# Second GINE layer held turned through two products, with a third product that brings its rows back without their mean

## Chip, cores and metric

The kernel runs on one core of a Trainium2 chip. The metric is the device time of one execution in microseconds (us), the median of several runs. Engines are called as the profile calls them: PE (TensorE, with PEld for its weight loads), DVE (VectorE), ACT (ScalarE), POOL (GpSimd) and SP (SyncE).

## What is computed

Four residual graph layers run over 100000 nodes of 96 channels with 50000 edges; each ends in a layer norm without gain or shift. The change touches the last layer, and of it the second convolution:

```python
def _layernorm(x, axis=-1, eps=1e-05):
    m = jnp.mean(x, axis=axis, keepdims=True)
    v = jnp.var(x, axis=axis, keepdims=True)
    return (x - m) / jnp.sqrt(v + eps)

def _gine_conv(x, src, dst, e, W1, b1, W2, b2):
    msg = jax.nn.relu(x[src] + e)
    agg = jax.ops.segment_sum(msg, dst, num_segments=x.shape[0])
    h = x + agg
    h = jax.nn.relu(h @ W1 + b1)
    h = jax.nn.relu(h @ W2 + b2)
    return h
...
h = _gine_conv(x, src, dst, e, W00, b00, W01, b01)
h = jax.nn.relu(h)
h = _gine_conv(h, src, dst, e, W10, b10, W11, b11)
h = jax.nn.relu(h)
...
x = _layernorm(x + h)      # this x is the output of the layer norm before
```

## The kernel before

Nodes without an incoming edge need no sums, so the dense rows of a layer ("base" rows) can be computed from the features alone. Rows of nodes with incoming edges ("slots", one for each edge, sorted by destination) are computed again with their sums and scattered over the dense ones. The last convolution runs in three stages.

- **First slots stage** (`slot_rows "gine1_slots"`): the slots of the first convolution, beside the lower half of the dense rows of the second. The change leaves it alone.
- **Gather stage** (`edge_pass "gine2"`, line 436): POOL issues 392 indirect DMAs (line 516), each of which fetches 128 rows of `conv`; seven make one of 56 batches, five batches are ahead, and eight buffers exist. DVE adds the edge features (`join`, line 534), ACT applies relu (line 633), DVE chains the rows into running sums in PSUM (line 582, eight instructions a batch), ACT copies the sums out (line 1887), SP stores them. When the last batch is chained, PE and ACT make one row of corrections (lines 602, 648, 651), which POOL adds by an indirect DMA (line 1944). Beside this each engine runs a share of a job: the upper half of the dense rows of the second convolution, class `GineRows`.
- **Last slots stage** (`slot_rows "gine2_slots"`): `GineRows` over 49 batches of 1024 slots, and POOL scatters each finished batch into the output with eight indirect DMAs (line 985).

`GineRows` (line 1159) works on half batches of 512 rows, step q on each engine in program order. PE transposes four tiles of 128 rows (line 1146, tile `turned`), ACT copies them to SBUF (line 1124), PE multiplies by the first weights with 512 columns (line 1242, `hidden`), ACT applies bias and relu (line 1227), and PE multiplies by the second weights so that the rows come back upright (line 1154, `product`, four matmuls of 96 columns; the bias rides on a row of ones). DVE takes relu and adds the skipped features (line 1208, `product` in PSUM, `skip` in SBUF). For each batch of two halves the norm follows: DVE sums the rows (line 1029) and subtracts the mean in one instruction on 768 elements whose two tensor inputs are both in SBUF (line 1031), ACT squares (line 1070), DVE sums the squares (line 1037), ACT takes the root (line 1076), DVE inverts it (line 1046), and the rows are scaled: with `scaled_by_act` by eight ACT instructions (line 1063), else by one DVE instruction with both inputs in SBUF (line 1050). In the slots DVE first adds the features to the sums, both in SBUF (line 1132), in odd steps:

```python
        if q % 2:
            self.add(ph, dve, (q + 3) // 2)
```

Before it writes a rows buffer again, DVE waits in `left` until the scatter of four batches ago has landed. The order of a stage is what the code issues: for every batch each engine runs its own work and then the job's steps that `share` gives to that batch (104 steps over 56 batches here).

## Time and profile before

| | us |
|---|---|
| median of 3 runs | 13920.73 (13897.24 to 13924.33) |
| profiled execution, its own time | 13921.51 |
| its span | 13919.8 |
| gather stage, first gather to last | 12807.52 to 13313.30 |
| last slots stage, first scatter to last | 13388.21 to 13916.7 |

The times of the timeline are counted from the start of the span. The gather stage and the last slots stage are the last 1112 us of the program.

### The profile page before, as it was taken

How to read it: one execution, taken by the hardware profiler on the slowest of the kernel's cores; microseconds unless marked ns; L12 is line 12 of the kernel's file. 1: busy time of each engine (PE TensorE's matmuls, PEld its weight loads, DVE VectorE, ACT ScalarE, POOL GpSimd, SP SyncE). 2: the span in 40 equal slices, each digit the busy share in tenths (PEclk: the TensorE clock that was granted, in tenths of full speed). 3: DMA queues.
4: the chain of work that ended last, by engine and by line, in shares of the span. 5: the costliest groups of instructions: out<-in, count | busy, mean ns of one | idle time of the engine just before them, and what ended most of it. 6: DMA issues, size and time to landing. Idle time of an engine off the chain costs nothing. (4 is left out here: it accounts for less than half of the span.)

```text
span 13919.8 us, 114314 instructions
## 1 busy us (share of the span) xinstructions
PE 5477.0 (39%) x29175; PEld 4357.4 (31%) x29175; DVE 7700.5 (55%) x13539; ACT 4324.3 (31%) x11110; POOL 8089.8 (58%) x8280
## 2 busy tenths in 40 slices
PE   0000002100000000210003877776778888988876
PEld 0000002000000000210002666654556887766544
DVE  8880245444444444542256255676755778567753
ACT  0000011100000000110046565466655246654654
POOL 0567777777777777777733773177765000721767
PEclk9965555555555555555556767987789988999555
DMA  7300124434334334431257544444467788876743
GB/s 227 117 4 3 36 78 137 123 113 119 113 113 119 113 113 119 127 107 53 55 187 239 167 142 132 148 141 126 138 212 244 233 288 316 269 252 227 227 165 111
DMA packets 955756, 2071.60 MB, mean 149 GB/s; under 512 B 318458, under 2 KB 323856, under 8 KB 938977
## 3 DMA queue, kind: packets, MB, share of 16 engines
q1 hardware_dynamic: 689376, 1702.87, 35.4%
q0 software_dynamic: 265728, 361.43, 11.6%
q8 instruction: 241, 3.95, 0.1%
q14 instruction: 411, 3.36, 0.1%
HBM read 1251.36 MB, written 822.13 MB: 149 GB/s over the span
## 5 line engine op out<-in xcount | busy, mean ns | idle before, releaser
L720 POOL DMA_INDIRECT hop_raw<-hop_table,i_hop x2352 | 2219.6, 944 | 734.5 <-issue 693.0
L814 PE MATMUL hop_rows<-hop_chain,src_carries 128*128 128x96 f32 x12 | 4.3, 450 | 3023.8 <-DVE hop_chain L790 3023.8
L744 DVE TENSOR_TENSOR hop_rows<-hop_raw,hop_factors 128x672 f32<-128x672 f32 x336 | 289.9, 863 | 1494.4 <-DMA hop_raw<-hop_table,i_hop 1494.4
L822 ACT ACTIVATE hop_keeps<-src_inner 128x672 f32<-128x672 f32 x336 | 255.4, 762 | 2665.2 <-DVE hop_chain L790 2613.1
L516 POOL DMA_INDIRECT gine_raw<-x,i_near x392 | 379.1, 967 | 1177.4 <-POOLq L89 1058.2
L516 POOL DMA_INDIRECT cheb_raw<-cheb_table,i_cheb x784 | 817.4, 1043 | 244.9 <-issue 235.9
L814 PEld LDWEIGHTS hop_rows<-hop_chain,src_carries 128*128 128x128 f32 x12 | 3.0, 312 | 3025.1 <-issue 3025.1
L516 POOL DMA_INDIRECT cheb_raw<-x,i_near x392 | 446.4, 1139 | 510.0 <-POOLq L89 390.8
L516 POOL DMA_INDIRECT gine_raw<-conv,i_near x392 | 387.6, 989 | 603.6 <-POOLq L89 484.5
L1784 POOL DMA_INDIRECT own_raw<-x,i_dst x392 | 370.1, 944 | 505.3 <-POOLq L89 386.2
L1621 PE MATMUL cheb_base_product<-folded,cheb_base_turned_rows 97*128 97x292 f32 x1568 | 561.9, 514 | 177.1 <-ACT cheb_base_mixed L1580 177.1
L790 DVE TENSOR_TENSOR_SCAN hop_chain<-hop_keeps,hop_rows 128x672 f32<-128x672 f32 x336 | 521.9, 1553 | 11.6
L985 POOL DMA_INDIRECT out_dram<-gine_slots_ends_rows,dst_end x392 | 410.3, 1047 | 154.5 <-issue 119.1
L299 POOL DMA_INDIRECT x_and_map<-sort_dst_entry,src_map_end x392 | 393.6, 1004 | 129.1 <-issue 128.2
L516 POOL DMA_INDIRECT gcn_raw<-x,dst_other x392 | 382.6, 976 | 131.0 <-issue 115.6
L299 POOL DMA_INDIRECT x_and_map<-fold_entry,dst_map_end x392 | 381.0, 972 | 127.8 <-issue 127.0
L2000 POOL DMA_INDIRECT hop_sums<-hop_last_sums,src_end x392 | 383.8, 979 | 119.4 <-issue 119.4
L1621 PEld LDWEIGHTS cheb_base_product<-folded,cheb_base_turned_rows 97*128 97x128 f32 x1568 | 354.0, 237 | 299.8 <-ACT cheb_base_mixed L1580 188.7
L720 POOL DMA_INDIRECT hop_first_raw<-x_and_map,src_other x392 | 369.9, 944 | 131.6 <-issue 119.2
L720 POOL DMA_INDIRECT hop_last_raw<-hop_table,i_hop x392 | 373.5, 953 | 122.5 <-issue 119.2
L720 POOL DMA_INDIRECT hop_second_raw<-hop_table,i_hop x392 | 369.9, 944 | 124.9 <-issue 113.4
L720 POOL DMA_INDIRECT hop_ninth_raw<-hop_table,i_hop x392 | 370.0, 944 | 122.4 <-issue 115.8
(560 smaller groups left out, 22128.9 us busy)
## 6 DMA issues: line engine op xcount, KB each, us to landing
hop_res<-hop_table SPq DMA_DIRECT2D x336, 336.0 KB
hop_table<-hop_sums SPq DMA_DIRECT2D x336, 336.0 KB, 2.3
part<-cheb_put_mixed SPq DMA_DIRECT2D x49, 1168.0 KB
cheb_slots_ends_part<-part SPq DMA_DIRECT2D x49, 1168.0 KB, 7.6
start_x_x<-x_and_map SPq DMA_DIRECT2D x98, 400.0 KB, 4.2
x<-start_x_rows SPq DMA_DIRECT2D x98, 400.0 KB, 4.0
cheb_base_term<-x SPq DMA_DIRECT2D x98, 400.0 KB, 3.7
mid<-cheb_base_rows SPq DMA_DIRECT2D x98, 400.0 KB
```

The source lines that it names most:

```text
L299: pool.indirect_dma_start(out=self.node_map, out_offset=bass.IndirectOffsetOnAxis(ap=side.map_end[:, t:t + 1], axis=0), in_=self.entry[:, ...
L516: pool.indirect_dma_start(out=raw_rows[:, b % RAW, g, :], out_offset=None, in_=table, in_offset=bass.IndirectOffsetOnAxis(ap=index[:, t:t ...
L720: pool.indirect_dma_start(out=raw_rows[:, b % RAW, g, :], out_offset=None, in_=table, in_offset=bass.IndirectOffsetOnAxis(ap=index[:, t:t ...
L744: nc.vector.tensor_tensor(by_channel(b).rearrange("p c t -> p t c"), raw[:, b % RAW, :, :], spread(weights[:, at], C), ALU.mult).then_inc( ...
L790: nc.vector.tensor_tensor_scan(line(chain), line(keeps), rows[b % LINES], 0.0, ALU.mult, ALU.add)\
L814: nc.tensor.matmul(carried, side.carries[:, :], chain[:, (batches - 1) % LINES, :, EDGE - 1], start=True, stop=True).then_inc(s["carried"], 1)
L822: nc.scalar.activation(keeps[:, b % LINES, :, :], side.inner[:, b * EDGE:(b + 1) * EDGE].unsqueeze(1).to_broadcast([P, C, EDGE]), ACT.Copy ...
L985: pool.indirect_dma_start(out=table, out_offset=bass.IndirectOffsetOnAxis(ap=side.end[:, t:t + 1], axis=0), in_=self.wide_rows[:, m, g, :] ...
L1621: ins = nc.tensor.matmul(into[:, start:], self.turned_rows[0:rows, q % 2, j, c, :], self.k.folded[0:rows, power, start:MIX], start=(j == 0 ...
L1784: pool.indirect_dma_start(out=raw[:, b % RAW, g, :], out_offset=None, in_=table, in_offset=bass.IndirectOffsetOnAxis(ap=index[:, t:t + 1], ...
L2000: pool.indirect_dma_start(out=self.out, out_offset=bass.IndirectOffsetOnAxis(ap=ph.edge["side"].end[:, t:t + 1], axis=0), in_=ph.edge["sum ...
```

## The change

Both later stages now use a new class, `CentredGineRows`; the dense rows of the lower half keep `GineRows`. After `hidden`, PE multiplies again with 512 columns, with the second weights as the stationary operand, so that the result stays turned (`second`, 96 x 512). ACT applies the second bias and relu (line 1323, `second_rows`). A third product (line 1154 again, four matmuls) brings the rows back upright, multiplied by `k.centring`, the identity less 1/96, which takes off each row's mean. The skipped features come out of a layer norm, so their mean is zero, and DVE adds them to the PSUM product with a plain add (line 1298). The row sum and the subtraction of the mean on DVE (lines 1029 and 1031) are gone. In the gather stage the scaling moves from eight ACT instructions to one DVE instruction (line 1050); in the slots ACT keeps it. Transposes run three steps ahead in place of two, loads three batches ahead in place of two, and in the gather stage `turned` and `hidden` have one PSUM bank each (`fronts=1`). In the slots the add of line 1132 moves to the start of the even step, ahead of the wait for the scatter.

```diff
+class CentredGineRows(GineRows):
+    signals = GineRows.signals + ("second", "bent")
+    LEAD = 3
...
+        self.steps = range(-3, 2 * self.count + self.tail)
...
+    def centre(self, ph, dve, i): pass
...
+    def vector(self, ph, dve, q):
+        i, m = q // 2, q // 2 % self.DEPTH
+        if q % 2 == 0:
+            self.add(ph, dve, q // 2 + 2)
+        if 0 <= q < 2 * self.count:
+            if q % 2 == 0 and i >= self.DEPTH:
+                self.left(ph, dve, i - self.DEPTH)
+            g0 = q % 2 * 4
+            self.landed(ph, dve, i)
+            dve.wait_ge(self.sem(ph, "product"), q + 1)
+            self.nc.vector.tensor_tensor(self.rows[:, m, g0:g0 + 4, :], self.product[q % self.banks][:, :, :],
+                                         self.tiles["skip"][:, m, g0:g0 + 4, :], ALU.add)\
+                .then_inc(self.sem(ph, "taken"), 1)
...
+    def scalar(self, ph, act, q):
+        nc, n, s, v = self.nc, 2 * self.count, q + 2, q + 1
+        self.copy(ph, act, q + 3, True)
+        if 0 <= s < n:
+            act.wait_ge(self.sem(ph, "hidden"), s + 1)
...
+            nc.scalar.activation(self.hidden_rows[:, s % 2, :, :], self.hidden[s % self.fronts][:, :, :], ACT.Relu,
+                                 bias=self.c0[:, 0:1]).then_inc(self.sem(ph, "activated"), 1)
+        if 0 <= v < n:
+            act.wait_ge(self.sem(ph, "second"), v + 1)
...
+            nc.scalar.activation(self.second_rows[:, v % 2, :, :], self.second[v % 2][:, :, :], ACT.Relu,
+                                 bias=self.c1[:, 0:1]).then_inc(self.sem(ph, "bent"), 1)
+        self.scalar_norm(ph, act, q)
...
+    def tensor(self, ph, pe, q):
+        n, h, u = 2 * self.count, q + 2, q + 1
+        self.turn(ph, pe, q + 3)
...
+        if 0 <= u < n:
+            pe.wait_ge(self.sem(ph, "activated"), u + 1)
...
+            self.nc.tensor.matmul(self.second[u % 2][:, :, :].rearrange("c g p -> c (g p)"), self.w1[:, :],
+                                  self.hidden_rows[:, u % 2, :, :].rearrange("c g p -> c (g p)"),
+                                  start=True, stop=True).then_inc(self.sem(ph, "second"), 1)
+        if 0 <= q < n:
+            pe.wait_ge(self.sem(ph, "bent"), q + 1)
+            self.multiply(ph, pe, q, self.second_rows, self.k.centring[:, :])
...
-                  jobs=(GineRows(nc, k, "base", True, high, conv, second, out, skip=x3, turned_by_act=True,
-                                scaled_by_act=True),))
-        slot_rows(nc, k, "gine2_slots", GineRows(nc, k, "ends", False, slots, conv_slots, second, None, sums=sums2,
-                                                 skip=x3_slots, scatter=(by_dst, out, k.N - 1),
-                                                 turned_by_act=True, scaled_by_act=True))
+                  jobs=(CentredGineRows(nc, k, "base", True, high, conv, second, out, x3, fronts=1),))
+        slot_rows(nc, k, "gine2_slots", CentredGineRows(nc, k, "ends", False, slots, conv_slots, second, None, x3_slots,
+                                                        sums=sums2, scatter=(by_dst, out, k.N - 1), scaled_by_act=True))
```

How this moves instructions shows at two places. The first is DVE in the last slots stage, one batch of two steps. It stood before, from the half that waits for the scatter:

```order
L1208 SCALAR_TENSOR_TENSOR gine_slots_ends_rows<-gine_slots_ends_product,gine_slots_ends_skip 128x384
L1029 TENSOR_REDUCE gine_slots_ends_total<-gine_slots_ends_rows 128x8
L1031 SCALAR_TENSOR_TENSOR gine_slots_ends_rows<-gine_slots_ends_total,gine_slots_ends_rows 128x768
L1046 RECIPROCAL gine_slots_ends_inverse<-gine_slots_ends_root 128x8
L1132 TENSOR_TENSOR gine_slots_ends_sums<-gine_slots_ends_sums,gine_slots_ends_x 128x768
L1208 SCALAR_TENSOR_TENSOR gine_slots_ends_rows<-gine_slots_ends_product,gine_slots_ends_skip 128x384
L1037 TENSOR_REDUCE gine_slots_ends_spread<-gine_slots_ends_square 128x8
```

The same place now:

```order
L1298 TENSOR_TENSOR gine_slots_ends_rows<-gine_slots_ends_product,gine_slots_ends_skip 128x384
L1046 RECIPROCAL gine_slots_ends_inverse<-gine_slots_ends_root 128x8
L1298 TENSOR_TENSOR gine_slots_ends_rows<-gine_slots_ends_product,gine_slots_ends_skip 128x384
L1037 TENSOR_REDUCE gine_slots_ends_spread<-gine_slots_ends_square 128x8
L1132 TENSOR_TENSOR gine_slots_ends_sums<-gine_slots_ends_sums,gine_slots_ends_x 128x768
```

Two instructions of 768 elements are gone, and the add of line 1132 stands last, behind the sum of squares.

The second place is ACT in the gather stage, one batch of the gather with two steps of the job. Before:

```order
L1124 ACTIVATE gine_base_turned_rows<-gine_base_turned 96x512
L1227 ACTIVATE gine_base_hidden_rows<-gine_base_hidden,gine_base_c 96x512
L1070 ACTIVATE gine_base_square<-gine_base_rows 128x768
L1887 ACTIVATE gine_sums<-gine_total 128x384
L1887 ACTIVATE gine_sums<-gine_total 128x288
L633 ACTIVATE gine_rows<-gine_raw 128x384
L633 ACTIVATE gine_rows<-gine_raw 128x288
L1124 ACTIVATE gine_base_turned_rows<-gine_base_turned 96x512
L1227 ACTIVATE gine_base_hidden_rows<-gine_base_hidden,gine_base_c 96x512
L1063 ACTIVATE gine_base_rows<-gine_base_rows,gine_base_inverse 128x96 x8
L1076 ACTIVATE gine_base_root<-gine_base_spread,gine_base_eps 128x8
```

Now:

```order
L633 ACTIVATE gine_rows<-gine_raw 128x384
L633 ACTIVATE gine_rows<-gine_raw 128x288
L1124 ACTIVATE gine_base_turned_rows<-gine_base_turned 96x512
L1317 ACTIVATE gine_base_hidden_rows<-gine_base_hidden,gine_base_c 96x512
L1323 ACTIVATE gine_base_second_rows<-gine_base_second,gine_base_c 96x512
L1070 ACTIVATE gine_base_square<-gine_base_rows 128x768
L1124 ACTIVATE gine_base_turned_rows<-gine_base_turned 96x512
L1317 ACTIVATE gine_base_hidden_rows<-gine_base_hidden,gine_base_c 96x512
L1323 ACTIVATE gine_base_second_rows<-gine_base_second,gine_base_c 96x512
L1076 ACTIVATE gine_base_root<-gine_base_spread,gine_base_eps 128x8
L1989 ACTIVATE gine_sums<-gine_total 128x384
```

The eight scalings are gone from ACT, and a relu of 512 columns (line 1323) stands in each step. Line 1989 is the former line 1887.

## Rows read from the trace of the kernel before

**Rows 1.** Busy time by window: gather stage, last slots stage (us, then engines)
```profile
core 0: us, PE busy (x) PEld busy (x) DVE busy (x) ACT busy (x) POOL busy (x), PEclk, DMA share, GB/s
12807.00:13316.00 509.00, 425.63 (x1351) 282.58 (x1352) 352.31 (x760) 322.76 (x855) 387.57 (x392) 0.52 0.70 222
13388.00:13917.00 529.00, 372.48 (x1260) 264.17 (x1260) 217.87 (x324) 245.49 (x658) 409.71 (x392) 0.57 0.35 121
```
**Rows 2.** Page, costliest groups: POOL's indirect DMAs, busy and mean ns
```profile
L720 POOL DMA_INDIRECT hop_raw<-hop_table,i_hop x2352 | 2219.6, 944 | 734.5 <-issue 693.0
...
L516 POOL DMA_INDIRECT gine_raw<-x,i_near x392 | 379.1, 967 | 1177.4 <-POOLq L89 1058.2
L516 POOL DMA_INDIRECT gine_raw<-conv,i_near x392 | 387.6, 989 | 603.6 <-POOLq L89 484.5
...
L985 POOL DMA_INDIRECT out_dram<-gine_slots_ends_rows,dst_end x392 | 410.3, 1047 | 154.5 <-issue 119.1
...
L516 POOL DMA_INDIRECT gcn_raw<-x,dst_other x392 | 382.6, 976 | 131.0 <-issue 115.6
```
**Rows 3.** Timeline of one slots batch, POOL, then DVE (start, us, engine)
```profile
13509.17 0.97 POOL L985 DMA_INDIRECT out_dram<-gine_slots_ends_rows,dst_end  x1 [0.30 <-issue]
13510.45 1.63 POOL L985 DMA_INDIRECT out_dram<-gine_slots_ends_rows,dst_end  x1 [0.30 <-issue]
...
13508.83 0.56 DVE L1208 SCALAR_TENSOR_TENSOR gine_slots_ends_rows<-gine_slots_ends_product,gine_slots_ends_skip 128x384 f32<-128x384 f32 x1 [5.62 <-DMA out_dram<-gine_slots_ends_rows,dst_end]
...
13510.28 0.96 DVE L1031 SCALAR_TENSOR_TENSOR gine_slots_ends_rows<-gine_slots_ends_total,gine_slots_ends_rows 128x768 f32<-128x768 f32 x1
```
**Rows 4.** Tile hop_factors, which is in PSUM: DVE's instructions on it
```profile
L744 DVE TENSOR_TENSOR hop_rows<-hop_raw,hop_factors x336: 861/862/864, 2600.3 to 5604.0; 128x672 f32<-128x672 f32 x168
```
**Rows 5.** Timeline of the gcn gather stage, DVE's scaling and POOL's gather
```profile
8159.24 0.96 DVE L1050 TENSOR_TENSOR gcn_base_rows<-gcn_base_rows,gcn_base_inverse 128x768 f32<-128x768 f32 x1
...
8159.39 1.62 POOL L516 DMA_INDIRECT gcn_raw<-x,dst_other  x1 [0.30 <-issue]
```
**Rows 6.** Timeline, end of the gather stage: last gather, ACT until the corrections
```profile
13313.30 0.94 POOL L516 DMA_INDIRECT gine_raw<-conv,i_near  x1 [0.30 <-issue]
...
13317.57 0.84 ACT L1070 ACTIVATE gine_base_square<-gine_base_rows 128x768 f32<-128x768 f32 x1 [3.80 <-DVE gine_base_rows L1031]
...
13319.37 2.22 ACT L1063 ACTIVATE gine_base_rows<-gine_base_rows,gine_base_inverse 128x96 f32<-128x96 f32 x8
...
13348.21 0.25 ACT L651 ACTIVATE gine_fix<-gine_total 128x96 f32<-128x96 f32 x1 [0.90 <-PE gine_total L602]
```
**Rows 7.** Timeline, end of the first convolution's gather stage, the same two points
```profile
12297.27 0.95 POOL L516 DMA_INDIRECT gine_raw<-x,i_near  x1 [0.30 <-issue]
...
12315.32 0.25 ACT L651 ACTIVATE gine_fix<-gine_total 128x96 f32<-128x96 f32 x1 [1.20 <-PE gine_total L602]
```
**Rows 8.** Timeline of PE, one half batch in the slots at the lower clock
```profile
13512.23 1.09 PE L1146 MATMUL gine_slots_ends_turned<-ident,gine_slots_ends_sums 128*96 128x128 f32 x4 [2.73 <-DVE gine_slots_ends_sums L1132]
13513.11 1.91 PE L1242 MATMUL gine_slots_ends_hidden<-e_slots_ends_turned_rows,gine_slots_ends_w 96*96 96x512 f32 x2
13514.82 1.86 PE L1154 MATMUL gine_slots_ends_product<-gine_slots_ends_w,e_slots_ends_hidden_rows 97*128 97x96 f32 x8
13516.47 1.06 PE L1146 MATMUL gine_slots_ends_turned<-ident,gine_slots_ends_sums 128*96 128x128 f32 x4
```
**Rows 9.** Timeline, start of the last slots stage: PE, ACT, POOL
```profile
13364.45 1.92 PE L1146 MATMUL gine_slots_ends_turned<-ident,gine_slots_ends_sums 128*96 128x128 f32 x8 [16.29 <-DVE gine_slots_ends_sums L1132]
...
13370.90 1.02 PE L1242 MATMUL gine_slots_ends_hidden<-e_slots_ends_turned_rows,gine_slots_ends_w 96*96 96x512 f32 x2
13371.76 1.03 PE L1154 MATMUL gine_slots_ends_product<-gine_slots_ends_w,e_slots_ends_hidden_rows 97*128 97x96 f32 x8
...
13388.21 1.73 POOL L985 DMA_INDIRECT out_dram<-gine_slots_ends_rows,dst_end  x1 [35.43 <-ACT gine_slots_ends_rows L1063]
```
**Rows 10.** Busy time by window, columns as in rows 1: first convolution's gather stage
```profile
11900.00:12300.00 400.00, 374.83 (x2216) 281.58 (x2215) 226.35 (x560) 256.00 (x493) 303.13 (x313) 0.92 0.83 273
```

58 lines of the change are left out of this document (52 added, 6 removed).

## Prediction

> **What bounds the kernel now.** I read the windows first. The two stages that the change touches take 509 and 529 us from first to last indirect DMA [rows 1], and in neither is any computing engine busy throughout: DVE 69% and 41%, ACT 63% and 46%, PE 84% and 70%, at a granted clock of 0.52 and 0.57, so mostly 1.2 of 2.4 GHz. Then the costliest groups. POOL's DMAs are issued one behind another with about 0.3 us between (the bracket of each row, [rows 3]); the only wait of the scatters for data is one of 35.4 us, before the first [rows 9]. So POOL sets the pace of both stages: 392 x (0.99 + 0.30) = 506 us and 392 x (1.05 + 0.30) = 529 us. What can be gained is not DVE or ACT time as such, but three other things: the time by which the gather stage ends behind its last gather, the time before the first scatter, and the length of POOL's own instructions.
>
> That last one varies, and the same groups show it. An indirect DMA costs 944 ns in the hop stages, but 967, 976 and 989 ns in gather stages with other work beside them, and 1047 ns in the last slots [rows 2], where an undisturbed one takes 0.97 us and one in each batch 1.63 [rows 3]. The timeline shows with what the long one coincides. Line 1031, which reads two tensors from SBUF, begins 0.17 us before it and runs 0.96 us, and POOL's instruction ends 0.66 us late. In the gcn stage line 1050, which also has both inputs in SBUF, does the same: 1.62 us in place of 0.94 [rows 5]. Line 744 has one input in PSUM and stands 336 times beside hop gathers [rows 4], whose mean is still 944 ns [rows 2]. So what stretches POOL is a DVE instruction with two SBUF inputs that is running when POOL's begins. Lines 1208 and the new 1298 read the product from PSUM and should cost nothing.
>
> **The change, part by part.** Four terms lie on the path.
>
> 1. *End of the gather stage.* The last gather begins at 13313.30, the corrections are ready at 13348.21, 34.9 us later [rows 6]. The consumers are some batches behind by then: ACT waits 3.80 us for the subtraction of the mean, then squares, scales for 2.22 us, and only then turns to the next gathered batch, while DVE waits for ACT [rows 6]. This ring of DVE (sum, mean: 2 x 0.95) and ACT (scaling: 2.22) is what the change opens: it takes 1.9 us off DVE and 2.2 off ACT a batch, and adds 0.96 for the scaling to DVE and two relus to ACT, whose like is one PSUM read of 512 columns each, under 0.7 us. In the first convolution's gather stage, whose job has no norm and so no such ring, the same two points are 18.0 us apart [rows 7]. I take that distance: 34.9 - 18.0 = **-17 us**. Bounds: nothing, if the consumers stay late for another reason, and -24, if they are within one batch (about 11 us: landing, join, relu, chain, sums).
>
> 2. *Length of the gathers.* Before, 392 x (989 - 944) ns = 17.6 us are lost [rows 2]. The 49 subtractions of line 1031 go, 49 scalings of line 1050 come, both with two SBUF inputs and 768 elements. The join of line 534 alone costs 392 x 23 ns = 9.0 us in the first convolution, and the gcn stage with 49 scalings of this form loses 392 x 32 ns = 12.5 us [rows 2]. Sum 21.5, less 17.6: **+4 us**. Bounds: the scaling never meets a starting gather (-9), or every one costs the 0.68 us of [rows 5]: 33 + 9 - 17.6 = +25.
>
> 3. *Length of the scatters.* Before, 392 x (1047 - 970) ns = 30 us are lost [rows 2, 3]. Line 1031 goes for good. What is left is line 1132, the add, with two SBUF inputs. DVE's order follows the landing of a scatter. After the wait it ran line 1208 at 13508.83 [rows 3]; now come 0.56, about 0.2, 0.56, 0.95 of the sum of squares with small gaps, so the add would begin some 2.2 us behind it, near 13511.0, and end near 13511.9. Without the stretch POOL would begin at 13510.45 and 13511.72, so the add reaches some 0.15 us into an instruction's beginning, of which in [rows 5] the first 0.14 or so are free (0.83 us after POOL's start the scaling ends, and the loss is 0.68). I leave 0.1 x 49 = 5 us: **-25 us**. Bounds: -30 (nothing left) and 0 (the add takes the place of line 1031 in full).
>
> 4. *Time to the first scatter.* PE begins at 13364.45 and POOL at 13388.21 [rows 9]. ACT scales batch 0 in step 5, behind seven relus of `second`, one more transposed half and one more `hidden`. A product of 512 columns takes 0.86 us there (13370.90 to 13371.76, so PE is already at 2.4 GHz), so 7 x 0.86 + 0.44 + 0.86 = 7.3 us more PE work; the row sum and mean of DVE (1.9 us) leave the path, and PE's waits for the add with them, since it now comes first. I take **+4 us**; bounds 0 (all hidden in waits) and +12 (PE at the lower clock, twice the price, less the same).
>
> What costs nothing: the third product is as large as the second before; 49 row sums and ACT's added relus (98 x 0.68 = 67 us against 109 us of scalings taken off in the gather stage) lie under POOL's 506 and 529 us. The second column load replaces a row load before the stage's nine first loads, a DMA issue among many. The third load ahead adds a wait on SP for DVE's last step; the store behind it in SP's queue is of a batch made earlier, and nobody on POOL waits for it.
>
> **TensorE is the cover that gets thin.** At 1.2 GHz a half batch takes 4.24 us (13512.23 to 13516.47), of which `hidden` is 1.71 [rows 8]; with `second` it is 5.95. 98 halves make 583 us, more than POOL's 506 and about 500. At 2.4 GHz it would be 2.16 + 0.86 = 3.0 us, 296 us in all. So the stages stay POOL's only if the clock rises. In the first convolution's gather stage PE handles 3.5 halves a batch, double the present share, and is busy 94% at a granted 0.92 [rows 10], and at the start of the last slots it reached the upper level 6 us after its first matmul, having worked without a pause [rows 9]. Against that stands the present gather stage: 84% busy at 0.52 [rows 1]. My reading is that with a queue that is never empty the clock rises, PE catches up, pauses and falls again, and on the mean keeps pace.
>
> **Sum**: -17 + 4 - 25 + 4 = -34 us. The profiled execution took 13921.5 us, the median is 13920.7, so both bases give 13887. Differences under 0.2% (28 us) can hardly be told from none here.
>
> **The rivals.**
> - *The tail stays* (0.22): ACT and DVE are lighter, but now PE, with three products and single banks for `turned` and `hidden`, keeps the consumers as late as before. For it: ACT waits for two matmul results a step in place of one. Against: the first convolution's job, PE-heavy too, ends 18 us behind. 0 + 4 - 25 + 4 = -17: 13904.
> - *DVE falls into step with POOL* (0.11): once the consumers follow POOL, each instruction of DVE meets the same point of a POOL instruction in every batch, as line 1031 does in [rows 3]. If line 1050 hits a start each time and the add of line 1132 too: -17 + 25 + 0 + 4 = +12: 13933. The Trainium skill has the rule that goes with it (SBUF — State Buffer, "Who interferes with whom"): a DVE instruction with two SBUF inputs contends with a GpSimd instruction that reads SBUF, and whichever starts first keeps the other out for its whole length. By that rule the 49 scalings, which this change puts beside the gathers, could cost their whole 0.96 us each, 47 in place of 33; [rows 5] shows 0.68 of it.
> - *TensorE stays at 1.2 GHz* (0.09), the slower side: it becomes the bound once a half costs more than 506/98 = 5.2 us, and 5.95 does. The gather stage then lasts 583 us in place of 506 plus most of the 34.9 us tail, +55; the slots end at 13364.45 + 583 plus one batch of scatters, +42: 14018. The skill speaks against it (TensorE: Matmul & The Clock Gate, "Why this matters for your kernels"): a TensorE kept continuously busy gets its full clock; [rows 1] shows 84% at 0.52, so nearly busy is not enough.
>
> **How the numbers follow.** The forecast has 0.58, with a range of its own from 13858 (-24 - 9 - 30 + 0 = -63) to 13902 (its terms half as good). Within it some five in six lie below 13893, the bound of faster; with a fifth of the tail rival that is 0.54. Slower, above 13949, is the clock rival and a small part of the second: 0.11. The rest, 0.35, is within 0.2%. The range for eight in ten goes from 13860 to 13934: it takes in the first two rivals and leaves out the clock rival and the outermost ends.
>
> **What would show it.** Right: scatters with a mean near 985 ns and 505 us from first to last; gathers near 1000 ns; the corrections within 20 us of the last gather; the first scatter 27 to 29 us after the first slots transpose; a clock between 0.6 and 0.9 in both stages, and POOL still without waits. Wrong: POOL waiting for ACT within a stage (PE too slow), scatters still 1.6 us once a batch beside line 1132, or a tail of 35 us with ACT waiting for `second`.

## The result and the profile after

The changed kernel takes 13877.02 us (median of 9 runs, 13866.72 to 13889.41), the kernel before 13921.39 (9 runs, 13897.24 to 13926.33). The ratio is 0.9968 with a 95% interval from 0.996 to 0.9977. That is 44 us or 0.32% less, clear of no change and inside the predicted range, and 10 us below the predicted 13887. The profiled execution took 13877.02 us, with a span of 13875.2.

The two windows first, in the order of [rows 1]: the gather stage, then the last slots stage, each from its first indirect DMA to its last, with the columns of that group.

```profile
12803.00:13313.00 510.00, 392.45 (x1568) 236.41 (x1568) 320.07 (x726) 289.98 (x603) 390.82 (x392) 0.80 0.70 223
13371.00:13872.00 501.00, 392.16 (x1439) 228.23 (x1436) 132.63 (x230) 302.91 (x747) 381.90 (x391) 0.74 0.38 128
```

TensorE has a product more for every half batch (1568 matmuls for 1351, 1439 for 1260), yet its busy time fell from 426 to 392 us in the first window and rose only from 372 to 392 in the second: the granted clock went from 0.52 and 0.57 to 0.80 and 0.74. ACT lost 33 us in the gather stage and gained 57 in the slots; DVE lost 32 and 85. The gather window is 1 us longer, the slots window 28 us shorter. POOL's groups say the same, beside [rows 2]:

```profile
L720 POOL DMA_INDIRECT hop_raw<-hop_table,i_hop x2352 | 2219.5, 944 | 734.5 <-issue 692.7
...
L516 POOL DMA_INDIRECT gine_raw<-conv,i_near x392 | 391.7, 999 | 604.2 <-POOLq L89 485.0
L985 POOL DMA_INDIRECT out_dram<-gine_slots_ends_rows,dst_end x392 | 382.9, 977 | 158.5 <-issue 119.1
```

The gathers went from 989 to 999 ns, the scatters from 1047 to 977, and the hop gathers, which the change leaves alone, stayed at 944. The timeline of one batch in the slots stage, POOL and then DVE, against [rows 3]:

```profile
13608.57 0.97 POOL L985 DMA_INDIRECT out_dram<-gine_slots_ends_rows,dst_end  x1 [0.30 <-issue]
13609.85 0.97 POOL L985 DMA_INDIRECT out_dram<-gine_slots_ends_rows,dst_end  x1 [0.30 <-issue]
13611.12 1.04 POOL L985 DMA_INDIRECT out_dram<-gine_slots_ends_rows,dst_end  x1 [0.30 <-issue]
...
13608.26 0.56 DVE L1298 TENSOR_TENSOR gine_slots_ends_rows<-gine_slots_ends_product,gine_slots_ends_skip 128x384 f32<-128x384 f32 x1 [7.23 <-DMA out_dram<-gine_slots_ends_rows,dst_end]
...
13609.50 0.95 DVE L1037 TENSOR_REDUCE gine_slots_ends_spread<-gine_slots_ends_square 128x8 f32<-128x768 f32 x1
13610.36 0.95 DVE L1132 TENSOR_TENSOR gine_slots_ends_sums<-gine_slots_ends_sums,gine_slots_ends_x 128x768 f32<-128x768 f32 x1
```

The instruction of 1.63 us is gone. The add of line 1132 begins 2.10 us behind the first take, DVE's instruction that takes a product out of PSUM (line 1298, before line 1208; forecast: 2.2), and ends at 13611.31, 0.19 us into POOL's next instruction, which takes 0.07 us more than 0.97. Lines 1298 and 1037 run at the start of other scatters and cost nothing.

The end of the gather stage, against [rows 6]: the last gather, ACT's wait, the last gathered rows in ACT, the corrections. The time from the first of these to the last is called the tail below.

```profile
13312.79 1.00 POOL L516 DMA_INDIRECT gine_raw<-conv,i_near  x1 [0.31 <-issue]
...
13314.58 0.30 ACT L1076 ACTIVATE gine_base_root<-gine_base_spread,gine_base_eps 128x8 f32<-128x8 f32 x1 [4.38 <-DVE gine_base_spread L1037]
...
13322.40 0.85 ACT L633 ACTIVATE gine_rows<-gine_raw 128x384 f32<-128x384 f32 x2
...
13327.27 0.25 ACT L651 ACTIVATE gine_fix<-gine_total 128x96 f32<-128x96 f32 x1 [0.89 <-PE gine_total L602]
```

From the last gather to the corrections it is now 14.5 us, where it was 34.9. ACT still waits 4.38 us, for the sum of squares this time, but it is no longer behind: the last gathered rows reach it at 13322.40, 9.6 us behind the last gather, where they came at 13340.74 before, 27.4 us behind it. The corrections follow 4.9 us later. The start of the slots, against [rows 9]:

```profile
13342.67 1.91 PE L1146 MATMUL gine_slots_ends_turned<-ident,gine_slots_ends_sums 128*96 128x128 f32 x8 [15.44 <-DVE gine_slots_ends_sums L1132]
...
13367.92 2.24 ACT L1063 ACTIVATE gine_slots_ends_rows<-gine_slots_ends_rows,gine_slots_ends_inverse 128x96 f32<-128x96 f32 x8
...
13371.10 1.03 POOL L985 DMA_INDIRECT out_dram<-gine_slots_ends_rows,dst_end  x1 [39.38 <-ACT gine_slots_ends_rows L1063]
```

From the first transpose to the first scatter 28.4 us, where 23.8 stood. Put together, in us, from the timelines of the two profiled executions:

| piece | before | after | difference | forecast |
|---|---|---|---|---|
| start of span to first gather of the stage | 12807.5 | 12802.9 | -4.6 | 0 |
| first gather to last | 505.8 | 509.9 | +4.1 | +4 |
| last gather to corrections | 34.9 | 14.5 | -20.4 | -17 |
| corrections to first transpose of the slots | 16.2 | 15.4 | -0.8 | 0 |
| first transpose to first scatter | 23.8 | 28.4 | +4.7 | +4 |
| first scatter to last | 528.5 | 501.0 | -27.5 | -25 |
| last scatter to end | 3.1 | 3.1 | 0 | 0 |

The sum is -44.6, the whole difference of the two spans. The first row is no effect of the change: the stages ahead are the same code, and over the executions profiled below this start lies anywhere from 12785 to 12821 us. The spans of single executions are therefore compared by their terms here, and kernels by their medians.

### The profile page after: what moved, and what is told of

Same layout as the page of the kernel before. It is cut to its first block and busy times, and to the rows that moved or that the text cites. A ratio compares the mean times of both kernels' runs of the same rounds, so it can differ in the third digit from the quotient of the medians.

```text
span 13875.2 us, 115044 instructions
## 1 busy us (share of the span) xinstructions
PE 5451.9 (39%) x29567; PEld 4258.7 (31%) x29567; DVE 7569.1 (55%) x13390; ACT 4336.8 (31%) x10914; POOL 8066.2 (58%) x8280
## 5 line engine op out<-in xcount | busy, mean ns | idle before, releaser
L985 POOL DMA_INDIRECT out_dram<-gine_slots_ends_rows,dst_end x392 | 382.9, 977 | 158.5 <-issue 119.1
L720 POOL DMA_INDIRECT hop_first_raw<-x_and_map,src_other x392 | 369.9, 944 | 131.6 <-issue 119.1
```

The lines of the kernel that those rows point to most:

```text
L720: pool.indirect_dma_start(out=raw_rows[:, b % RAW, g, :], out_offset=None, in_=table, in_offset=bass.IndirectOffsetOnAxis(ap=index[:, t:t ...
L985: pool.indirect_dma_start(out=table, out_offset=bass.IndirectOffsetOnAxis(ap=side.end[:, t:t + 1], axis=0), in_=self.wide_rows[:, m, g, :] ...
```

## The experiments

My theory was that three of the four terms have causes that can be taken apart: the tail is the ring of DVE and ACT, the scatters are a matter of DVE instructions with two SBUF inputs, and the second product is hidden. The rivals were that PE keeps the tail, that the clock fails, and that DVE falls into step with POOL. In each diff the lines are those of the changed kernel, unless the text says that they start from the kernel before.

### One stage at a time

`gather_only` keeps the old class in the slots:

```diff
-        slot_rows(nc, k, "gine2_slots", CentredGineRows(nc, k, "ends", False, slots, conv_slots, second, None, x3_slots,
-                                                        sums=sums2, scatter=(by_dst, out, k.N - 1), scaled_by_act=True))
+        slot_rows(nc, k, "gine2_slots", GineRows(nc, k, "ends", False, slots, conv_slots, second, None, sums=sums2,
+                                                 skip=x3_slots, scatter=(by_dst, out, k.N - 1),
+                                                 turned_by_act=True, scaled_by_act=True))
```

> The new class in the gather stage alone, the last slots stage as before. If the terms add up as read: the gathers last about 4 us longer than before, the tail from last gather to corrections shrinks from 34.9 to about 14.5 us, and the scatter stage keeps its 529 us and 1047 ns a scatter: about 16 us less than before in all, 0.12%. Rival (the time before was lost through load on DVE and ACT in general, which the two stages share in effect): the scatters get faster too. Rival (the clock that is left high by the gather stage carries over): the first scatter comes earlier than 23.8 us after PE's first slots transpose.

Median 13896.91 us against 13916.32 of the kernel before on the same chip, ratio 0.9987 [0.9978, 0.9996]. The tail is 15.0 us, the gathers 995 ns, the scatters as before:

```profile
L516 POOL DMA_INDIRECT gine_raw<-conv,i_near x392 | 390.2, 995 | 604.2 <-POOLq L89 485.0
L985 POOL DMA_INDIRECT out_dram<-gine_slots_ends_rows,dst_end x392 | 410.1, 1046 | 155.1 <-issue 119.1
```

`slots_only` keeps the old class in the gather stage:

```diff
-                  jobs=(CentredGineRows(nc, k, "base", True, high, conv, second, out, x3, fronts=1),))
+                  jobs=(GineRows(nc, k, "base", True, high, conv, second, out, skip=x3, turned_by_act=True,
+                                scaled_by_act=True),))
```

> The new class in the last slots stage alone, the gather stage as before. Port theory: the scatters fall from 1047 to about 977 ns and from 528.5 to about 501 us, the first scatter comes 4.7 us later, tail and gathers as before (34.9 us, 989 ns): about 23 us less than before, 0.17%. Together with the gather part alone the two sums should give the 39 to 44 us of both. Rival (the stages depend on each other): the sum misses by over 8 us.

Median 13890.86, ratio 0.9984 [0.9975, 0.9993]. The tail is 33.6 us, the gathers 991 ns, the scatters 977 ns and 501.1 us from first to last. So each term belongs to its own stage. The gains add as well, 13916.32 - 13896.91 = 19.4 and 13916.32 - 13890.86 = 25.5, together 44.9, where both parts at once gave 44 us in one set of runs and 39 in another; but the intervals of the two ratios are some 25 us wide each, so this sum alone would not exclude an exchange of several us between the stages. The first slots transpose comes 24.7 us before the first scatter in `gather_only` and 27.0 in `slots_only`, so the start of the slots owes the change between 2.3 and 4.7 us.

### The ring of DVE and ACT

The ring is this: ACT waits for DVE's mean before it squares, DVE waits for ACT's gathered rows before it chains them, and each batch goes round both. The change opens it at two points: no mean on DVE, no scaling on ACT. Three kernels take the two apart. `act_scales` is the change with the scaling given back to ACT in the gather stage:

```diff
-                  jobs=(CentredGineRows(nc, k, "base", True, high, conv, second, out, x3, fronts=1),))
+                  jobs=(CentredGineRows(nc, k, "base", True, high, conv, second, out, x3, fronts=1, scaled_by_act=True),))
```

> The changed kernel with the scaling in the gather stage back on ACT in eight instructions, so that line 1050 is gone. Port theory: the gathers lose only what the join costs them, about 9 us in place of 22, mean near 967 ns, so the last gather comes about 12 us earlier; ACT's 2.2 us a batch may put 2 to 6 us on the tail. Net 6 to 10 us less than the changed kernel, 13868. Rival (ACT is what held the consumers): the tail goes back towards 30 us and the time rises by 5 or more.

`before_dve_scales` is the kernel before with the scaling given to DVE:

```diff
-                  jobs=(GineRows(nc, k, "base", True, high, conv, second, out, skip=x3, turned_by_act=True,
-                                scaled_by_act=True),))
+                  jobs=(GineRows(nc, k, "base", True, high, conv, second, out, skip=x3, turned_by_act=True),))
```

> The kernel before with the scaling in the gather stage on DVE (line 1050) in place of ACT. Ring theory: the ring of DVE and ACT loses 2.2 us of ACT and gains 0.96 us of DVE, from 10.5 to about 9.3 us, near POOL's pace, so that the tail falls from 34.9 to 18 to 26 us; port theory: lines 1031 and 1050 both meet gathers, and these last 8 to 15 us longer than 505.8. Sum within 8 us of the kernel before. Rival (only the subtraction of the mean holds the consumers): tail stays above 32 us, time 8 us or more above before.

`before_no_mean` is the kernel before with lines 1029 and 1031 left out, so that part of the computation is missing. The flag of the diff is set for the job of the gather stage alone:

```diff
+            if getattr(self, "uncentred", False):
+                dve.sem_inc(self.sem(ph, "centred"), 1)
+                return
             self.own.step(nc.vector.tensor_reduce(total, rows, AX_X, ALU.add))
```

> The kernel before, and in the gather stage the mean is neither computed nor taken off (lines 1029 and 1031 left out there), all else as before. Ring theory: DVE's 1.9 us leave the ring, which falls from 10.5 to 8.6 us, under POOL's pace, so the tail falls from 34.9 to 14 to 18 us. Port theory: 49 instructions with two SBUF inputs fewer, the gathers last 8 to 12 us less than 505.8. Together 25 to 32 us less than before. Rival (the 2.2 us of ACT are what holds the consumers): tail above 28 us.

| kernel | mean on DVE | scaling on | tail, us | gathers, ns | first gather to last, us | median, us | ratio |
|---|---|---|---|---|---|---|---|
| before | yes | ACT | 34.9 | 989 | 505.8 | 13921.39 | 1 |
| `before_no_mean` | no | ACT | 17.5 | 969 | 498.1 | 13893.1 | 0.9984 [0.9975, 0.9994] |
| `before_dve_scales` | yes | DVE | 19.6 | 1015 | 515.9 | 13905.76 | 0.9994 [0.9984, 1.0003] |
| `act_scales` | no | ACT | 17.6 | 956 | 493.1 | 13859.36 | 0.9965 [0.9951, 0.9979] |
| after | no | DVE | 14.5 | 999 | 509.9 | 13877.02 | 0.9968 [0.996, 0.9977] |

Each ratio is against the kernel before in the same set of runs.

The tail of `before_no_mean`, the same two points:

```profile
13305.55 0.94 POOL L516 DMA_INDIRECT gine_raw<-conv,i_near  x1 [0.30 <-issue]
...
13323.00 0.25 ACT L651 ACTIVATE gine_fix<-gine_total 128x96 f32<-128x96 f32 x1 [0.89 <-PE gine_total L602]
```

Either point alone brings the tail from 34.9 to below 20 with the old products, and the first does so with the new ones too. In `before_no_mean` ACT has as much to do as before, and in `before_dve_scales` DVE has more; neither engine's load alone explains both. That is the ring: once one link is shorter, the consumers are in time, and opening the second link gives only 2 to 5 us more. The waits of the gather stage say it too. DVE's wait for ACT's gathered rows, then its wait for the landing of a gather (us in total, times, longest), in the kernel before:

```profile
DVE gine_total L582 <- ACT gine_rows L633: 81.7, 45, 2.7
...
DVE gine_raw L534 <- DMA gine_raw<-conv,i_near: 40.3, 10, 12.2
```

And the same two in the changed one:

```profile
DVE gine_raw L534 <- DMA gine_raw<-conv,i_near: 126.4, 37, 13.5
...
DVE gine_total L582 <- ACT gine_rows L633: 14.0, 17, 1.5
```

DVE has caught up with POOL 10 times before and 37 times after, 53 times in `before_no_mean` and 25 in `before_dve_scales`. `before_no_mean` is 20 us faster by the medians (13913.21 - 13893.1) where 25 to 32 were expected. Its tail is as expected, and its gathers, 7.7 us shorter, are at the edge of the 8 to 12.

The price of the two points is not alike. Both versions that scale on DVE have gathers of 999 and 1015 ns, those that scale on ACT 956 and 969 (and 989 with the subtraction). `act_scales` gives back 3 us of tail and gains 17 us of gathers. `before_dve_scales` can't be told from no change: what it gains in the tail, its gathers cost. But the scaling itself is the smaller part of that. Only 4 gathers begin with line 1050 running, for 3.0 us; line 1031 costs 16.0 us in place of 14.3 and the joins of line 534 9.0 in place of 3.6, because they stand elsewhere against POOL's starts.

To see whether the scaling on ACT is really worth having, it ran again beside the change itself, on one chip. `changed_again` is the changed kernel, with no edit:

> The changed kernel itself, on the chip of the runs beside it, so that the kernel with ACT's scaling and the others have it to stand against. 40 to 48 us less than before, with the terms of its first profile within 4 us each: gathers 510, tail 14.5, start of the slots 28.4, scatters 501.

> The changed kernel with ACT's eight scalings in the gather stage, a second time and on the same chip as the changed kernel. If the gain is the length of the gathers: gathers near 493 us against 510, tail 3 us longer, 10 to 16 us less than the changed kernel. Rival (the first difference came from the stages before the gather stage, whose time varies from run to run): within 6 us of the changed kernel.

`changed_again` has a median of 13873.77 us, ratio 0.997 [0.9959, 0.9981], and `act_scales_again`, with the edit of `act_scales`, 13866.88, 0.9969 [0.9957, 0.998]. The gathers of the two, in that order:

```profile
L516 POOL DMA_INDIRECT gine_raw<-conv,i_near x392 | 388.7, 992 | 604.1 <-POOLq L89 484.9
```
```profile
L516 POOL DMA_INDIRECT gine_raw<-conv,i_near x392 | 381.6, 974 | 604.0 <-POOLq L89 484.8
```

The sign is the same, the size is not: 18 ns or 7 us in place of 43 ns or 17. The first time more was gained than the 6 to 10 us expected, the second time less than the 10 to 16. The medians are 7 us apart and the intervals overlap, so it is the best version by both medians, but its lead over the change isn't settled. Why the size moves can be read in the timelines. I sorted every gather by the DVE instruction at its start and summed what it took beyond 0.94 us. In `act_scales_again` the joins of line 534 cost 12 us, in `act_scales` 5, in the changed kernel 9, with 12 to 13 more for line 1050 (7 and 12 in `changed_again`). The code around the join is the same. Only its place against POOL's starts differs from one execution to the next.

### What stretches POOL in the slots

`add_late` gives the add of line 1132 back its old place, in the odd step behind the wait for the scatter:

```diff
-        if q % 2 == 0:
-            self.add(ph, dve, q // 2 + 2)
+        if q % 2 and q > -3:
+            self.add(ph, dve, (q + 3) // 2)
```

> The changed kernel with the add of the sums in the slots back in the odd step, behind the wait for the scatter, as before. Port theory: it then begins about 0.7 us after the first half is taken and ends just before POOL's next instruction begins, so the scatters stay near 972 to 990 ns and the time within 5 us. Rival (the freeing of PE's transposes from the scatter wait made the gain): the scatters go back to 1047 ns or POOL waits, 20 us or more. PE's idle time before the transposes in the slots should return, over 100 us, without effect.

This expectation failed. The median is 13963.53 us, ratio 1.0032 [1.002, 1.0044]: slower than the kernel before, and some 87 us above the changed one (13963.53 - 13877.02, another set of runs), and the scatters take 569 us from first to last in place of 501. Their mean length, 1006 ns, explains 392 x 29 ns = 11 us of that. The rest is in the view of waits of the last slots stage (us in total, times, longest):

```profile
DVE gine_slots_ends_rows L1298 <- PE gine_slots_ends_product L1154: 301.7, 67, 6.3
...
POOL out_dram L985 <- ACT gine_slots_ends_rows L1063: 111.5, 29, 51.6
ACT e_slots_ends_turned_rows L1124 <- PE gine_slots_ends_turned L1146: 107.5, 44, 4.8
PE gine_slots_ends_turned L1146 <- DVE gine_slots_ends_sums L1132: 105.2, 44, 5.2
```

51.6 us of POOL's wait for the scaling are the start of the stage (39.38 in the changed kernel). The rest is new. With what the same view puts down to "issue" POOL is idle between the scatters for 115.7 + 111.5 - 51.6 = 175.6 us, where 119.1 are the usual 0.30 each; the other 57 and the 11 make the 68. The transposes wait for the add, which now stands behind DVE's wait for a scatter; ACT's copy waits for the transposes; and the scaling that POOL waits for stands behind that copy in ACT's order. As these waits have it, each batch waits for the scatters of an earlier one through four engines. Line 1298 shows it from the other end: here DVE waits for PE's product 67 times, in the changed kernel's slots it waits for a scatter 45 times, for 324.2 us. PE's wait for the add is no news by itself, for in the kernel before it stands with 111.5 us in 43 waits, and POOL never waits there. What is new is a third product and a transpose that runs three steps ahead in place of two, which takes a step from between add and transpose. And the half batch behind the wait runs at the lower clock level: 5.94 us at a granted 0.50 (window 13609:13615), where the changed kernel takes 4.77. How the 57 us divide between these, no run separates. The move of the add, to which I had given no value but its place against POOL, is what lets the longer chain run at POOL's pace. The same kernel shows the stretch in the open; DVE, then POOL:

```profile
13608.33 0.91 DVE L1132 TENSOR_TENSOR gine_slots_ends_sums<-gine_slots_ends_sums,gine_slots_ends_x 128x768 f32<-128x768 f32 x1
```
```profile
13608.38 1.70 POOL L985 DMA_INDIRECT out_dram<-gine_slots_ends_rows,dst_end  x1 [0.30 <-issue]
```

The add is running when POOL's instruction begins, and that takes 1.70 us.

`extra_two` and `extra_one` add work on data of its own to DVE, once a batch behind the first take: a row sum of 768 elements and then either an addition of two SBUF tensors of that size, or a second row sum. Whatever the added time of DVE does, it does in both. What differs is whether the second instruction has two SBUF inputs. The edit of `extra_two` without the tiles that it adds, and the line in which `extra_one` differs:

```diff
+        if self.sums is not None and q % 2 == 0 and 0 <= i < self.count:
+            self.own.wait()
+            self.own.step(self.nc.vector.tensor_reduce(self.extra_sum[:, :], self.extra[:, 0, :, :], AX_X, ALU.add))
+            self.own.step(self.nc.vector.tensor_tensor(self.extra[:, 2, :, :], self.extra[:, 0, :, :], self.extra[:, 1, :, :], ALU.add))
...
-            self.own.step(self.nc.vector.tensor_tensor(self.extra[:, 2, :, :], self.extra[:, 0, :, :], self.extra[:, 1, :, :], ALU.add))
+            self.own.step(self.nc.vector.tensor_reduce(self.extra_sum2[:, :], self.extra[:, 1, :, :], AX_X, ALU.add))
```

> The changed kernel, and in each batch of the last slots DVE does two instructions more, where the row sum and the subtraction of the mean stood before: a row sum of 768 elements and then an addition of 768 elements with both inputs in SBUF, on tiles that nothing else uses. Port theory: one scatter in each batch becomes 0.65 us longer again, mean near 1045 ns in place of 977, the scatters take about 530 us in place of 501, and the time rises by 27 us or more. Rival (it is only DVE's load): the same as in the kernel with two row sums, at most a few us.

> The changed kernel, and in each batch of the last slots DVE does two row sums of 768 elements more, at the same place, each with one SBUF input, as long as the two instructions of the other kernel within 0.05 us. Port theory: scatters stay at 972 to 985 ns and 501 to 505 us; the time before the first scatter may grow by 2 us. Rival (DVE's load is what counts): scatters at 1040 ns, 27 us more.

`extra_two`: scatters of 1034 ns and 523.5 us from first to last, median 13900.68 us, ratio 0.9992 [0.9982, 1.0001]. That is 24 and 27 us above the two medians of the changed kernel; 1045 ns, 530 us and 27 or more were expected. Sorted by DVE's instruction at their start, its scatters lose 24.6 us, of which 23.9 with the added addition running, 0.54 us each in 44 meetings. In one batch, DVE's added instruction (line 1312) and POOL:

```profile
13607.74 0.95 DVE L1312 TENSOR_TENSOR gine_slots_ends_extra<-gine_slots_ends_extra 128x768 f32<-128x768 f32 x1
```
```profile
13608.00 1.53 POOL L985 DMA_INDIRECT out_dram<-gine_slots_ends_rows,dst_end  x1 [0.30 <-issue]
```

`extra_one`: scatters of 1022 ns, median 13893.0 us, ratio 0.9986 [0.9976, 0.9995]. I had expected 972 to 985 ns, and this missed too. The reason is in the same table: its scatters lose 19.6 us, all of it in 42 meetings with line 1132, 0.47 us each. The row sums stand at POOL's starts as often and cost nothing, but they move the add by nearly a microsecond, onto a start. DVE's two instructions, then POOL's two:

```profile
13604.86 0.94 DVE L1312 TENSOR_REDUCE ine_slots_ends_extra_sum<-gine_slots_ends_extra 128x8 f32<-128x768 f32 x1
...
13607.35 0.95 DVE L1132 TENSOR_TENSOR gine_slots_ends_sums<-gine_slots_ends_sums,gine_slots_ends_x 128x768 f32<-128x768 f32 x1
```
```profile
13605.13 0.97 POOL L985 DMA_INDIRECT out_dram<-gine_slots_ends_rows,dst_end  x1 [0.30 <-issue]
...
13607.68 1.46 POOL L985 DMA_INDIRECT out_dram<-gine_slots_ends_rows,dst_end  x1 [0.30 <-issue]
```

A reduction with one input runs over POOL's start and POOL takes its 0.97; an add with two inputs does it, and POOL takes 1.46. The two kernels are as good as one experiment on the kind of instruction, read batch by batch, though their totals (8 us apart) don't separate it. The size follows one rule in all these rows: POOL loses what DVE still had to run at POOL's start, less 0.12 or 0.13 us. In the slots of `add_late`, `extra_one` and `extra_two` this holds for each of the 119 scatters that began with more than 0.2 us of such an instruction left. It has an edge. In the gather stages of ten executions (the kernel before, the changed one twice, seven others), 39 gathers begin within 0.043 us of the start of such an instruction and lose nothing; the 23 that begin 0.045 to 0.09 us behind it lose 0.64 to 0.79 us. So the worst place and a free one are hardly 0.01 us apart.

| DVE's instruction | left at POOL's start, us | POOL's loss, us |
|---|---|---|
| line 1132, `add_late` | 13609.24 - 13608.38 = 0.86 | 1.70 - 0.97 = 0.73 |
| line 1050, gcn stage [rows 5] | 8160.20 - 8159.39 = 0.81 | 1.62 - 0.94 = 0.68 |
| line 1031, before [rows 3] | 13511.24 - 13510.45 = 0.79 | 0.66 |
| line 1312, `extra_two` | 13608.69 - 13608.00 = 0.69 | 0.56 |
| line 1132, `extra_one` | 13608.30 - 13607.68 = 0.62 | 0.49 |
| line 1132, after | 13611.31 - 13611.12 = 0.19 | 0.07 |

### TensorE as the bound

`double_second` issues the second product twice into the same bank, in both stages, which adds 512 columns to every half batch:

```diff
+            self.nc.tensor.matmul(self.second[u % 2][:, :, :].rearrange("c g p -> c (g p)"), self.w1[:, :],
+                                  self.hidden_rows[:, u % 2, :, :].rearrange("c g p -> c (g p)"),
+                                  start=True, stop=True)
```

> The changed kernel with each product `second` computed twice over in both stages, so that PE has 512 columns more for each half batch. At 1.2 GHz a half would cost 7.66 us, 751 us for 98; at 2.4 GHz 3.9 us, 380 us. Clock theory: the granted clock rises further, to 0.9 or so in both stages, gathers and scatters keep 510 and 501 us, the time before the first scatter grows by 6 us and the tail by up to 3: about 9 us more. Rival (PE is at its limit and the clock does not follow): POOL waits for ACT within the stages, and the time rises by over 50 us.

Median 13882.45 us, ratio 0.9975 [0.9966, 0.9985]: 5 and 9 us above the two medians of the changed kernel. The gathers take 998 ns, the tail 15.0 us, the scatters 977 ns, and the first scatter comes 33.5 us behind the first transpose, 5.1 later. The 98 added products of each stage cost nothing else that can be seen:

```profile
12821.00:13330.00 509.00, 431.69 (x1764) 242.95 (x1764) 319.01 (x721) 291.33 (x603) 390.05 (x391) 0.90 0.71 224
13396.00:13897.00 501.00, 411.59 (x1627) 225.56 (x1625) 132.89 (x230) 301.74 (x747) 382.07 (x391) 0.87 0.38 128
```

`second_four_times` issues it four times, with three products more than the changed kernel:

> The changed kernel with each product `second` computed four times over. At 2.4 GHz a half batch then costs PE 3.0 + 3 x 0.86 = 5.6 us, 549 us for 98, over POOL's 510 and 501. Clock theory with PE as the bound from here on: granted clock above 0.95 in both stages, gather stage and tail together 40 us or more longer, first scatter 18 us later, scatters 549 us, so 90 to 120 us more than the changed kernel. Rival (the four products one behind another cost less, or some other wait holds): under 60 us.

Median 13997.4 us, ratio 1.0061 [1.0045, 1.0076], 124 us above `changed_again` on the same chip, just over the 90 to 120 expected. Here TensorE is the bound, and at its upper clock level. Its windows of the two stages, and one of 400 us within the first:

```profile
12804.00:13322.00 518.00, 497.95 (x1936) 262.39 (x1937) 285.33 (x643) 267.80 (x541) 380.48 (x392) 0.97 0.65 203
13454.00:13997.00 543.00, 506.20 (x1992) 268.08 (x1990) 139.00 (x231) 306.85 (x748) 380.93 (x391) 0.97 0.35 119
```
```profile
12900.00:13300.00 400.00, 400.00 (x1577) 211.90 (x1575) 232.04 (x519) 215.94 (x438) 294.81 (x302) 1.00 0.66 207
```

POOL now waits for ACT in the slots, the tail is 72.0 us, the first scatter comes after 45.6 us and the last 542.7 behind it. From the first gather to the corrections it is 517.8 + 72.0 = 589.8 us, close to the 583 that the clock rival had for one product more at the lower level; it takes three more to get there.

## Why the prediction was right

**The bound.** POOL sets the pace of both stages before and after. Each of its instructions is followed by 0.30 us in both kernels, whatever the other engines do; it waits for more than that only in `second_four_times`, where PE is full, and in `add_late`.

**Term 1, the tail: -20.4 us measured, -17 forecast.** The reading that a ring of DVE and ACT kept the consumers late holds: three kernels that open it at one point or another have tails of 17.5, 19.6 and 17.6 us. The first convolution's 18.0 [rows 7] was a good likeness. The step was a little small, because both links were opened at once; the bound of -24 took that in. What I didn't see is that one link would have done. Executions with the same gather stage have tails of 13.8 to 15.0 us, so the 14.5 is no accident.

**Term 2, the gathers: +4.1 us measured, +4 forecast.** The sum of two sources was right and so was its split: line 534 costs 9 us, as forecast from the first convolution, and line 1050 12 to 13, as forecast from the gcn stage. But the agreement to a tenth is luck. The same kernel gave 992 ns and 507.0 us in `changed_again`, so +1.2, and `add_late`, whose gather stage is the same code, 515.7, so +9.9. Nor did the difference come about as the term reads. Before, line 1031 cost 14.3 us and the joins 3.6, so that swapping it for line 1050 gave 1.6 us, and the joins, whose code the change leaves alone, took 5.7 more.

**Term 3, the scatters: -27.5 us measured, -25 forecast.** Line 1031 was the cause: sorted by DVE's instruction at their start, the scatters lose 25.7 us to it before, and 3.8 to line 1132. Without it they are at 977 ns, and line 1132 costs 0.04 us a batch, 1.9 in all, where I had left 5. That 5 was a margin: by the step's own working (0.15 us into POOL's instruction, the first 0.14 free) next to nothing was due. The scaling in [rows 5] ends 0.81 us behind POOL's start, not 0.83 as I read it, which makes the free part 0.13. In the batch shown above the add reaches 0.19 us in. `extra_one` shows that this was near the edge. One more microsecond of DVE ahead of the add, and 19.6 us of it come back.

**Term 4, the start: +4.7 us measured, +4 forecast.** `double_second` prices it: 5.1 us for one more product a half batch. The working was 7.3 us of new PE work, less the 1.9 that DVE no longer does and some waits. Over the executions the new slots code gave 27.0 to 29.2 us and the old 23.8 to 24.7, so the size is known to a microsecond or two.

**What the sum left out.** -4.6 us lie before the first gather of the stage, in unchanged stages whose length moves from one execution to the next, and -0.8 between corrections and slots. The medians give 44 in the first set of runs and 39 in another (13913.21 - 13873.77); the forecast was 34. And the move of the add was costed by its place against POOL alone. `add_late` shows that it is worth some 80 us (68 between first scatter and last, 11.5 before the first): had it been left where it was, the kernel would have been slower than before. The prediction was right about the time and incomplete about why the new chain keeps pace.

**TensorE.** The cover got thinner and held. The clock came out at 0.80 and 0.74, inside the 0.6 to 0.9 that I had named. (At the start of the slots I read the upper level 6 us behind PE's first matmul from [rows 9]; the trace of before has a `hidden` of 1.02 us at 13368.73 already, 4.3 us behind it. Nothing in the sum hangs on it.) Within one batch of the slots it can be seen to rise; PE, from one batch's transposes to the next half's:

```profile
13601.09 0.84 PE L1146 MATMUL gine_slots_ends_turned<-ident,gine_slots_ends_sums 128*96 128x128 f32 x4 [1.30 <-DVE gine_slots_ends_sums L1132]
13601.73 1.94 PE L1337 MATMUL gine_slots_ends_hidden<-e_slots_ends_turned_rows,gine_slots_ends_w 96*96 96x512 f32 x2
13603.46 1.69 PE L1344 MATMUL gine_slots_ends_second<-e_slots_ends_hidden_rows,gine_slots_ends_w 96*96 96x512 f32 x2
...
13605.86 0.60 PE L1146 MATMUL gine_slots_ends_turned<-ident,gine_slots_ends_sums 128*96 128x128 f32 x4
13606.30 1.02 PE L1337 MATMUL gine_slots_ends_hidden<-e_slots_ends_turned_rows,gine_slots_ends_w 96*96 96x512 f32 x2
13607.16 1.02 PE L1344 MATMUL gine_slots_ends_second<-e_slots_ends_hidden_rows,gine_slots_ends_w 96*96 96x512 f32 x2
```

The first half batch begins behind a wait and runs its products `hidden` and `second` at the lower level (1.94 us for the first), the second, which follows without a pause, at the upper (1.02). The granted clock is 0.59 from 13601.0 to 13605.2 and 1.00 from 13605.8 to 13608.2.

**The rivals.** *The tail stays* fell with the 14.5 us, and with `double_second`, where PE has four products a half batch and the tail is 15.0. *DVE in step with POOL* fell too, but its mechanism is real: in `add_late` and `extra_one` the add does stretch a scatter in 34 and 41 of the 49 batches. In the changed kernel it misses, and the scalings of line 1050 hit only some of their starts, because the gather stage's DVE isn't tied to one POOL instruction. The rule that went with it (the Trainium skill, SBUF — State Buffer, "Who interferes with whom") calls the port pair that DVE and GpSimd share an exclusive lock, says that a DVE instruction with two SBUF inputs contends with a GpSimd instruction that reads SBUF, and that the order of issue decides who blocks; that the other waits for the whole instruction it says of DVE's two-port modes, and the prediction put the two together. These traces agree by half: POOL is held as the table above has it, but DVE isn't. In the changed kernel's gather stage the scaling of line 1050 begins 19 times within half a microsecond behind a gather's start, takes 0.96 or 0.97 us each time, and the gather its 0.94 or 0.95. One of them, DVE and POOL:

```profile
13067.57 0.96 DVE L1050 TENSOR_TENSOR gine_base_rows<-gine_base_rows,gine_base_inverse 128x768 f32<-128x768 f32 x1
```
```profile
13067.42 0.94 POOL L516 DMA_INDIRECT gine_raw<-conv,i_near  x1 [0.30 <-issue]
```

*TensorE stays at 1.2 GHz* fell at 0.80. That PE becomes the bound once a half batch costs it more than POOL's time is right, as `second_four_times` shows at the upper level; what a whole stage costs at the lower level no run shows. The rule named against it (the Trainium skill, TensorE: Matmul & The Clock Gate, "Why this matters for your kernels": a TensorE kept continuously busy gets the full clock) agrees with the fourfold product: 400.00 us busy of 400 at 1.00.

## What to carry to other kernels

Where POOL's indirect DMAs set the pace, look at what DVE is running when each of them begins: an instruction with two SBUF inputs costs POOL nearly what is left of it, one with an input in PSUM or with one input costs nothing in these traces, so a subtraction that can be folded into a matrix product is worth its POOL time even if DVE has time to spare. When a chain gets a stage longer, move whatever feeds its head ahead of every wait for its tail: in `add_late` no engine is busy for more than 420 of the 569 us, and the order inside DVE costs the 87. And a ring of two engines is opened by its cheaper link: here ACT had room for the scaling and POOL had none for DVE's.

## What I had not expected of the hardware

- The granted clock followed the work without costing any. In the gather stage it was 0.52 before, 0.80 after, 0.90 with the second product doubled and 0.97 with it fourfold, while first gather to last took 506, 510, 509 and 518 us. PE's busy time moved far less than its work (426, 392, 432 and 498 us): most of the new work went into a faster clock. A high busy share at 0.52 says little of how near PE is to being the bound.
- What a DVE instruction costs POOL is a matter of tenths of a microsecond in its place. The add of line 1132 costs 0.04 us a batch in the changed kernel, 0.47 with two row sums ahead of it; and the joins cost 5 us in one execution and 12 in another of the same kernel, and the changed kernel's gather stage took from 507 to 516 us from first gather to last over six executions. Differences under some 10 us in a gather stage are therefore not evidence for an edit without several runs.
- One place of one instruction in a queue (`add_late`) was worth about twice the whole gain of the change.
